# A two-layer graph kernel: a new order of work in the attention stage, and one pair's key rows gathered

## The chip, the cores and the metric

The kernel runs on one core of a Trainium2 chip. The metric is the device time of one execution in microseconds (us). A core has a matrix engine (PE, with its weight loads shown apart as PEld), a vector engine (DVE), a scalar engine (ACT), GpSimd (POOL), and a sync engine (SP) that here only issues transfers. Each works through its own list of instructions in order; they meet at semaphores.

## The reference

A graph of 3125 nodes with 256 features and 50,000 edges sorted by destination goes through two layers.

```python
h = relu(layernorm(x))
x = x + attention_layer(h)     # 8 heads of 32
h = relu(layernorm(x))
x = x + relation_layer(h)      # 8 relations
# attention_layer: q, k, v = layernorm(h) @ Wqkv + b
#   e = exp(q[src] . k[dst] - max),  agg = segment_sum(v[src] * e / sum(e), dst)
#   x1 = h + agg;  x1 + gelu(layernorm(x1) @ W_in + b_in) @ W_out + b_out
# relation_layer: sum over edges into dst of (h @ W[type])[src], + h @ loop_w + bias, gelu, layernorm
```

## The kernel before, in words

Nodes are cut into 25 blocks of 128. Edges are cut into 49 visits (`v`) of 1024, eight tiles of 128 edges; two tiles are a pair (`j` is 0 to 3). There are three stages, each a block of five instruction lists written out by hand. What stands in those lists sets the order of the work; there is no planner.

The first stage (to about 140 us) normalizes x, computes q, k and v for each block of nodes and writes tables to memory: `qv_tab` (q and v, float32, L263) and `k_tab` (the key cut into three bfloat16 parts, L265). DVE's `take` (L560) empties the products from PSUM, POOL's `split_keys` makes the three parts.

The second stage (about 140 to 1000 us) is the fused one, which the change is about. For each visit it does the edge work:
- POOL's `gather` (L1088): eight indirect transfers that fetch the q and v rows of the edges' sources. They wait until the same pair of the visit before last has been summed.
- PE's `keys(v, j)` (L1267): the key rows of a pair's destinations, by an indicator matrix times a window of 128 rows of `k_tab`, six bfloat16 matmuls into two PSUM banks. Pairs 0 and 2 use banks 0 and 1, pairs 1 and 3 banks 2 and 3, so each waits until the scores of the last user of its banks are ready.
- DVE: the product of q and key rows (L1500), its sum per head (L1505), `weigh` of the pair before (L1431, v times exponential) and `shift` (L1424). `to_window` (L1415) makes the indicators of the next visit.
- ACT's `weights(v, j)` (L1147, the exponentials), and `indicators` (L1138), which copies the indicators that PE's `turn` (L1257) has transposed.
- PE's `add_up(v, j)` (L1282) sums a pair into its window of nodes, `carry` (L1293) adds the last window's overlap, ACT's `take` (L1131) empties the result, SP stores it.

Into this the work on blocks of nodes is woven, one block `m` per two visits from visit 4 on. In even visit v = 4 + 2m (`hid`): DVE's `prepare` and `normalize` (L1440, L1459), PE's `turn_y`, ACT's `y_features`, PE's `hidden` in two halves (L1313), ACT's eight gelus in two halves (`gelu`, L1161). In odd visit v + 1 (`out`): PE's `feed` (L1325, the product with W_out), DVE's `statistics` (L1469) and `scale_of` (L1481), ACT's `relu` (L1170), PE's `turn_h1` (L1332), ACT's `h1_features` (L1180), then PE's `message` 0 to 3 (L1338, the products with eight relation matrices) and ACT's `keep_messages` (L1185). Messages 2 and 3 fall into the next even visit (`old`). ACT needs one table for the gelus and one for the exponentials; each change of table is an ACT_TABLE_LOAD. The lists of the two visits are in the loops at L1193 (ACT), L1351 (PE) and L1492 (DVE).

After visit 48 the last blocks are finished; a third stage (from about 1000 us) gathers the messages.

## Time and profile before

| what | value |
|---|---|
| median of three timed runs | 1618.47 us (1613.39 to 1624.01) |
| the profiled execution, its own time | 1609.75 us |
| its span in the trace | 1607.9 us |
| PE busy | 1168.3 us (73%) |
| DVE busy | 908.4 us (56%) |
| POOL busy | 889.5 us (55%) |
| ACT busy | 454.6 us (28%) |
| granted PE clock, mean | 0.876 of full |

Busy time is summed over the whole span, over stages with different limits. The chain of waits on the page follows only the end of the third stage, so the fused stage has to be read from its own rows.

### The profile page before, as it was taken

Reading aid. Unit: us, or ns where it says so; the run is one execution under the profiler, and the core shown is the slowest. Engines: PE = TensorE matmul, PEld = TensorE weight load, DVE = VectorE, ACT = ScalarE, POOL = GpSimd, SP = SyncE. Lnnn points to the kernel's source line nnn. Section 1 sums busy time; section 2 is a strip of 40 time slices with the busy share of each in tenths; the row PEclk is TensorE's granted clock in tenths of the full one; section 3 lists DMA queues with packets and bytes.
Section 4 is the critical chain, followed back from the end, with each engine's and each line's share of the span. In section 5 each row is a group of like instructions: output and inputs, shape, how many; then the busy total and the mean of one; then the engine's idle time right before and its main releaser. Section 6 shows DMA issues by size and latency. Waiting matters only on the chain. (4 is left out here: it accounts for less than half of the span.)

```text
span 1607.9 us, 18550 instructions
## 1 busy us (share of the span) xinstructions
PE 1168.3 (73%) x5463; PEld 864.7 (54%) x5463; DVE 908.4 (56%) x2801; ACT 454.6 (28%) x1150; POOL 889.5 (55%) x959
## 2 busy tenths in 40 slices
PE   5874579999899989999899988354565645553662
PEld 2443466777667766777667755233344424442452
DVE  5664577767777777777777662113434324533534
ACT  4652134443444443453444433000000000000000
POOL 2655656555555455555555510566676667666760
PEclk9997799999999999999999999687777767776776
DMA  6648666666667666566666611233343334433431
GB/s 203 157 132 265 208 200 201 205 222 202 207 197 233 206 210 188 189 223 189 203 191 220 194 46 57 79 108 106 113 125 114 114 106 121 119 115 109 121 114 51
DMA packets 137073, 255.68 MB, mean 159 GB/s; under 512 B 40426, under 2 KB 85460, under 8 KB 134026
## 3 DMA queue, kind: packets, MB, share of 16 engines
q0 software_dynamic: 50176, 154.19, 32.3%
q1 hardware_dynamic: 85834, 99.10, 19.0%
q10 hardware_dynamic: 960, 1.18, 0.2%
q8 instruction: 45, 0.74, 0.2%
q14 instruction: 58, 0.48, 0.1%
HBM read 192.76 MB, written 61.63 MB: 158 GB/s over the span
## 5 line engine op out<-in xcount | busy, mean ns | idle before, releaser
L1093 POOL DMA_INDIRECT arena<-qv_tab,srcs x392 | 391.8, 999 | 349.1 <-PE ps L1289 252.1
L1687 POOL DMA_INDIRECT arena<-h_all,typs x392 | 377.2, 962 | 210.3 <-issue 135.2
L1751 PE MATMUL ps<-arena 128*128 128x256 f32 x784 | 252.7, 482 | 114.8 <-DMA arena<-h_all,typs 49.9
L1289 PE MATMUL ps<-arena 128*128 128x264 f32 x784 | 221.2, 406 | 88.8 <-DVE arena L1437 49.9
L1751 PEld LDWEIGHTS ps<-arena 128*128 128x128 f32 x784 | 186.6, 246 | 176.1 <-issue 40.6
L1289 PEld LDWEIGHTS ps<-arena 128*128 128x128 f32 x784 | 140.2, 194 | 139.3 <-DVE arena L1437 66.8
L1500 DVE TENSOR_TENSOR arena<-arena,ps 128x512 f32<-128x512 f32 x196 | 134.3, 685 | 119.5 <-PE ps L1278 91.5
L1344 PE MATMUL ps<-wrel,arena 128*128 128x512 f32 x400 | 188.7, 598 | 1.7 <-ACT arena L1182 1.7
L1278 PE MATMUL ps<-arena 128*128 128x264 bf16 x1176 | 169.6, 282 | 12.6 <-DMA arena<-k_tab 11.0
L1278 PEld LDWEIGHTS ps<-arena 128*128 128x128 bf16 x1176 | 145.0, 145 | 41.4 <-issue 25.3
L1437 DVE TENSOR_TENSOR arena<-arena 128x512 f32<-128x512 f32 x196 | 134.0, 684 | 41.6 <-ACT arena L1150 40.9
L1505 DVE TENSOR_REDUCE arena<-arena 128x16 f32<-128x512 f32 x196 | 134.2, 685 | 5.1
L1804 DVE TENSOR_TENSOR arena<-ps,rowb 128x256 f32<-128x256 f32 x25 | 10.6, 425 | 223.7 <-remote 170.0
L1701 ACT ACTIVATE arena<-ps 128x256 f32<-128x256 f32 x49 | 18.7, 383 | 415.6 <-remote 286.5
L1150 ACT ACTIVATE arena<-arena,nbias 128x16 f32<-128x16 f32 x196 | 60.4, 308 | 196.4 <-DVE arena L1428 183.6
L1344 PEld LDWEIGHTS ps<-wrel,arena 128*128 128x128 f32 x400 | 73.1, 192 | 58.1 <-issue 52.4
L1189 ACT ACTIVATE arena<-ps 128x512 f32<-128x512 f32 x100 | 59.8, 598 | 137.9 <-PE ps L1344 125.0
L1328 PE MATMUL ps<-wout,arena 128*128 128x256 f32 x400 | 92.5, 385 | 6.0 <-issue 3.3
L1320 PEld LDWEIGHTS ps<-arena,win 128*128 128x128 f32 x800 | 93.0, 192 | 2.3 <-issue 0.5
L1788 DVE TENSOR_SCALAR arena<-dstf,wst 128x8 f32<-128x8 f32 x49 | 11.3, 230 | 145.9 <-ACT arena L1701 78.9
L1320 PE MATMUL ps<-arena,win 128*128 128x128 f32 (+1 forms) x800 | 93.2, 275 | 0.0
L1733 PE MATMUL ps<-ident,arena 128*128 128x128 f32 x50 | 14.8, 392 | 105.4 <-DVE arena L1799 82.5
(162 smaller groups left out, 1521.1 us busy)
## 6 DMA issues: line engine op xcount, KB each, us to landing
h_all<-arena SPq DMA_DIRECT2D x23, 1024.0 KB
arena<-dst SPq DMA_DIRECT2D x49, 256.0 KB
rel<-arena SPq DMA_DIRECT2D x77, 128.0 KB
arena<-k_tab SPq DMA_DIRECT2D x49, 198.0 KB
att<-arena SPq DMA_DIRECT2D x52, 132.0 KB, 6.0
qv_tab<-arena SPq DMA_DIRECT2D x25, 256.0 KB, 3.1
arena<-qv_tab,srcs POOLq DMA_INDIRECT x392
arena<-h_all,typs POOLq DMA_INDIRECT x392
```

Source lines behind the costliest of these rows:

```text
L1093: pool.indirect_dma_start(out=rowbuf[:, u * T + t, 0:2 * D], out_offset=None, in_=qv_tab, in_offset=bass.IndirectOffsetOnAxis(ap=srcs[:, v ...
L1150: nc.scalar.activation(rowbuf[:, at:at + 2, 2 * D:2 * D + H], sco[:, 2 * j:2 * j + 2, :], ACT.Exp, bias=nbias[:, :], scale=SCALE).then_inc ...
L1278: last = nc.tensor.matmul(ps[:, t % 4, 0:KW], tiles[:, t, :], kwin[:, u, c * KW:(c + 1) * KW], start=(c == 0), stop=(c == 2))
L1289: last = nc.tensor.matmul(ps[:, AGG, 0:AW], ind[:, v % 2, t, :], rowbuf[:, v % 2 * T + t, D:2 * D + H], start=(t == 0), stop=(v == 0 and t ...
L1320: last = nc.tensor.matmul(ps[:, (bank_y(m), bank_x(m))[half], n * P:n * P + wide_m], win[:, k, f * 128:(f + 1) * 128], yT[:, m % 2, k, 0:w ...
L1328: last = nc.tensor.matmul(ps[:, bank_y(m), 0:D], gT[:, m % 2, f, :], wout[:, f, :], start=(f == 0), stop=(f == FF // 128 - 1))
L1344: last = nc.tensor.matmul(ps[:, (bank_y(m), bank_x(m))[c % 2], :], h1T[:, m % 2, k, :], wrel[:, k, c * 512:(c + 1) * 512], start=(k == 0), ...
L1437: nc.vector.tensor_tensor(vals, vals, b[:, :, 2 * D:2 * D + H].unsqueeze(3).broadcast_to([EP, 2, H, DH]), ALU.mult).then_inc(w_ready, 1)
L1500: own.did(nc.vector.tensor_tensor(b[:, :, 0:D], b[:, :, 0:D], ps[:, bank:bank + 2, 0:D], ALU.mult))
L1505: own.did(nc.vector.tensor_reduce(sco[:, 2 * j:2 * j + 2, :], b[:, :, 0:D].rearrange("p t (h d) -> p t h d", d=DH), AX.X, ALU.add))
L1687: pool.indirect_dma_start(out=rowbuf[:, u * T + t, :], out_offset=None, in_=h_all[0:N * R, :], in_offset=bass.IndirectOffsetOnAxis(ap=typs ...
L1751: last = nc.tensor.matmul(ps[:, 6 + u, 0:D], ind[:, u, t, :], rowbuf[:, u * T + t, :], start=(t == 0), stop=(v == 0 and t == T - 1))
```

## The change

The fused stage's lists are written in another order, and the key rows of pair 1 of each odd visit no longer come from PE: POOL gathers them, float32, from a new table `kf_tab`, into a tile `kg`.

- First stage: `kf` (the ring of four key tiles) gets 8 more columns, which hold zeros, and SP stores each tile to `kf_tab` between the two stores that were there. `take` waits for all three stores of the block four before it, since the tile is now read by a store.
- PE: an odd visit is now add_up 0, add_up 1, feed, keys(next, 0), turn(next), add_up 2, keys(next, 1), add_up 3. The even visit begins with the odd visit's carry, then turn_h1 and messages 0 and 1; messages 2 and 3 follow in it. keys 2 and 3 of the next odd visit stand before the second half of `hidden`.
- ACT: the odd visit keeps only weights 2 and 3 and the indicators; its weights 0 and 1 stand in the even visit ahead of both gelu halves. relu, h1_features and all four messages stand in the even visit, as does the even visit's `take`, ahead of the gelus.
- DVE: prepare goes from pair 0 to 1, normalize from 1 to 2, statistics from 1 to 3. weigh of an odd visit's pair 3 stands between statistics and scale_of instead of in the next visit.
- POOL: two more gathers in each odd visit, behind the fourth row gather; the residual additions move in between the next visit's row gathers.

```diff
@@ stage 1: SP, DVE @@
                     sp.wait_ge(qkv_taken, 2 * b + 1)
                     sp.dma_start(qv_tab[b * P:(b + 1) * P, :], ...).then_inc(stored[j], 16)
+                    sp.wait_ge(qkv_taken, 2 * b + 2)
+                    sp.dma_start(kf_tab[b * P:(b + 1) * P, :], kf[:, b % NK, :]).then_inc(stored[j], 16)
                     sp.wait_ge(kl_ready, b + 1)
...
                     if b >= NK:
+                        dve.wait_ge(stored[(b - NK) % NST], 48 * ((b - NK) // NST) + 48)
@@ fused stage @@
+            def gathered(v, j):
+                return v % 2 == 1 and j == 1
@@ POOL, gather(v) @@
+                        if t % 2 and gathered(v, t // 2):
+                            gather_keys(v, t // 2)
+                        if t == 3 and v >= 1 and out_of(v - 1) is not None:
+                            residual(out_of(v - 1))
+                        if t == 5 and before(v):
+                            shift_result(before(v) - 1)
+
+                def gather_keys(v, j):
+                    if v >= 2:
+                        pool.wait_ge(k_used, PAIRS * (v - 2) + j + 1)
+                    for t in (2 * j, 2 * j + 1):
+                        pool.indirect_dma_start(
+                            out=kg[:, t % 2, :], out_offset=None, in_=kf_tab,
+                            in_offset=bass.IndirectOffsetOnAxis(ap=dsti[:, v * T + t:v * T + t + 1], axis=0)
+                        ).then_inc(kg_in, 16)
@@ ACT @@
+                    if v % 2:
+                        weights(v, 2)
+                        weights(v, 3)
+                        indicators(v + 1)
+                        continue
...
                     if v + 1 < G:
                         indicators(v + 1)
+                        weights(v + 1, 0)
+                    take(v)
+                    if v + 1 < G:
+                        weights(v + 1, 1)
                     if hid is not None:
                         gelu(hid, 0)
                         gelu(hid, 1)
@@ PE, keys(v, j) @@
+                    if gathered(v, j):
+                        return
...
+                    last_user = PAIRS * v + j - 2
+                    if last_user >= 0 and gathered(last_user // PAIRS, last_user % PAIRS):
+                        last_user -= 2
@@ DVE @@
+                def key_rows(v, j):
                     bank = 2 * (j % 2)
+                    return kg if gathered(v, j) else ps[:, bank:bank + 2, 0:KW]
...
-                        if out is not None and j == 1:
-                            statistics(out)
-                        if out is not None and j == 2:
-                            scale_of(out)
+                        if v % 2 and j == 3:
+                            if out is not None:
+                                statistics(out)
+                            weigh(v, 3)
+                            if out is not None:
+                                scale_of(out)
```

PE before, from the feed of an odd visit (L1328) on: L1278 is keys, L1289 add_up, L1263 turn, L1335 turn_h1.

```order
L1328 MATMUL ps<-wout,arena 128x256 [waits hidden_ready]
L1328 MATMUL ps<-wout,arena 128x256 x7
L1278 MATMUL ps<-arena 128x264 [waits scores_ready]
L1278 MATMUL ps<-arena 128x264 x5
L1289 MATMUL ps<-arena 128x264 [waits osum_ready,ind_ready,weighted_ready]
L1289 MATMUL ps<-arena 128x264
L1278 MATMUL ps<-arena 128x264 [waits scores_ready]
L1278 MATMUL ps<-arena 128x264 x5
L1289 MATMUL ps<-arena 128x264 [waits ind_ready,weighted_ready]
L1289 MATMUL ps<-arena 128x264
```

PE in the changed kernel, from the second half of hidden (L1356) in an even visit, through the odd visit: L1325 is add_up, L1364 feed, L1314 keys, L1294 turn.

```order
L1356 MATMUL ps<-arena,win 128x128 x8
L1325 MATMUL ps<-arena 128x264 [waits osum_ready,ind_ready,weighted_ready]
L1325 MATMUL ps<-arena 128x264
L1325 MATMUL ps<-arena 128x264 [waits ind_ready,weighted_ready]
L1325 MATMUL ps<-arena 128x264
L1364 MATMUL ps<-wout,arena 128x256 [waits hidden_ready]
L1364 MATMUL ps<-wout,arena 128x256 x7
L1314 MATMUL ps<-arena 128x264 [waits scores_ready,key_window_in0,indT_ready]
L1314 MATMUL ps<-arena 128x264 x5
L1294 MATMUL ps<-identb,arena 128x128 [waits ind_ready]
L1294 MATMUL ps<-identb,arena 128x128 x7
```

Two add_ups now stand between the hidden products and the feed, and keys 2 and 3 of the odd visit are gone from behind the feed. What follows in the changed kernel is the boundary to the even visit: L1337 is the carry, L1371 turn_h1, L1380 the messages.

```order
L1325 MATMUL ps<-arena 128x264 [waits ind_ready,weighted_ready]
L1325 MATMUL ps<-arena 128x264
L1337 MATMUL ps<-arena 128x264 [waits car_ready,osum_ready]
L1371 MATMUL ps<-ident,arena 128x128 [waits h1_ready]
L1371 MATMUL ps<-ident,arena 128x128
L1380 MATMUL ps<-wrel,arena 128x512 [waits h1T_ready]
L1380 MATMUL ps<-wrel,arena 128x512 x3
L1325 MATMUL ps<-arena 128x264 [waits osum_ready,ind_ready,weighted_ready]
```

There is now nothing on PE between the carry, turn_h1 and the first messages; before, a keys group and an add_up stood between turn_h1 and message 0.

ACT before, around the gelus (L1166): L1150 is an exponential, L1136 take, L1143 the indicators, L1174 relu.

```order
L1143 ACTIVATE arena<-ps 128x512 [waits summed,turn_ready]
L1143 ACTIVATE arena<-ps 128x512
L1166 ACT_TABLE_LOAD
L1166 ACTIVATE arena<-ps,bin_ 128x128 [waits hidden_psum]
L1166 ACTIVATE arena<-ps,bin_ 128x128 x3
L1166 ACTIVATE arena<-ps,bin_ 128x128 [waits hidden_psum]
L1166 ACTIVATE arena<-ps,bin_ 128x128 x3
L1150 ACT_TABLE_LOAD
L1150 ACTIVATE arena<-arena,nbias 128x2x8 [waits scores_ready]
L1136 ACTIVATE arena<-ps 128x264 [waits att_out,window_done]
L1150 ACTIVATE arena<-arena,nbias 128x2x8 [waits scores_ready] x2
```

The same place in the changed kernel (L1169 indicators, L1176 exponential, L1162 take, L1192 gelu).

```order
L1169 ACTIVATE arena<-ps 128x512
L1176 ACTIVATE arena<-arena,nbias 128x2x8 [waits scores_ready]
L1162 ACTIVATE arena<-ps 128x264 [waits att_out,window_done]
L1176 ACTIVATE arena<-arena,nbias 128x2x8 [waits scores_ready]
L1192 ACT_TABLE_LOAD
L1192 ACTIVATE arena<-ps,bin_ 128x128 [waits hidden_psum]
L1192 ACTIVATE arena<-ps,bin_ 128x128 x3
L1192 ACTIVATE arena<-ps,bin_ 128x128 [waits hidden_psum]
L1192 ACTIVATE arena<-ps,bin_ 128x128 x3
L1176 ACT_TABLE_LOAD
L1176 ACTIVATE arena<-arena,nbias 128x2x8 [waits scores_ready] x2
```

Two exponentials and the take moved from behind the gelus to ahead of them.

## Rows read from the trace of the kernel before

**Rows 1.** The page's head, and stretches: busy (instructions) per engine, PEclk, DMA share, GB/s.
```profile
span 1607.9 us, 18550 instructions
...
180.00:220.00 40.00, 25.81 (x139) 20.46 (x139) 29.89 (x69) 7.68 (x21) 24.85 (x27) 0.91 0.74 229
...
400.00:500.00 100.00, 90.62 (x509) 70.24 (x510) 74.90 (x202) 42.61 (x100) 55.51 (x58) 1.00 0.66 207
```

**Rows 2.** Timeline of PE, the hidden products of the second and the last pair of visits.
```profile
255.53 3.73 PE L1320 MATMUL ps<-arena,win 128*128 128x128 f32 x32
...
946.39 3.84 PE L1320 MATMUL ps<-arena,win 128*128 128x128 f32 x32
```

**Rows 3.** Timeline of PE, one pair of visits: start, length, line, [idle before <- releaser].
```profile
502.95 1.16 PE L1289 MATMUL ps<-arena 128*128 128x264 f32 x4 [1.67 <-issue]
503.94 0.38 PE L1335 MATMUL ps<-ident,arena 128*128 128x128 f32 x2
...
513.84 1.88 PE L1344 MATMUL ps<-wrel,arena 128*128 128x512 f32 x4
515.56 1.05 PE L1289 MATMUL ps<-arena 128*128 128x264 f32 x4
516.45 0.84 PE L1278 MATMUL ps<-arena 128*128 128x264 bf16 x6
517.12 0.38 PE L1310 MATMUL ps<-ident,arena 128*128 128x128 f32 x2
...
518.78 3.73 PE L1320 MATMUL ps<-arena,win 128*128 128x128 f32 x32
522.36 0.84 PE L1278 MATMUL ps<-arena 128*128 128x264 bf16 x6
...
524.80 3.72 PE L1328 MATMUL ps<-wout,arena 128*128 128x256 f32 x16 [0.27 <-ACT arena L1166]
...
531.77 1.16 PE L1289 MATMUL ps<-arena 128*128 128x264 f32 x4 [1.02 <-DVE arena L1437]
```

**Rows 4.** Timeline of DVE, the same pair of visits.
```profile
504.96 0.17 DVE L1444 TENSOR_SCALAR arena<-arena 128x8 f32<-128x8 f32 x1
...
509.41 0.15 DVE L711 TENSOR_SCALAR arena<-arena 128x1 f32<-128x1 f32 x1
...
512.93 0.68 DVE L1500 TENSOR_TENSOR arena<-arena,ps 128x512 f32<-128x512 f32 x1
...
514.25 0.68 DVE L1437 TENSOR_TENSOR arena<-arena 128x512 f32<-128x512 f32 x1
...
528.56 0.42 DVE L1473 TENSOR_TENSOR xs<-xs,ps 128x256 f32<-128x256 f32 x1 [0.99 <-PE ps L1328]
...
529.71 0.69 DVE L1500 TENSOR_TENSOR arena<-arena,ps 128x512 f32<-128x512 f32 x1
...
531.72 0.15 DVE L696 TENSOR_SCALAR arena<-arena 128x1 f32<-128x1 f32 x1
...
533.71 0.69 DVE L1500 TENSOR_TENSOR arena<-arena,ps 128x512 f32<-128x512 f32 x1
```

**Rows 5.** Timeline of ACT, the same pair of visits.
```profile
504.36 0.39 ACT L1182 ACTIVATE arena<-ps 128x256 f32<-128x256 f32 x1 [0.78 <-PE ps L1335]
...
522.56 2.18 ACT L1166 ACTIVATE arena<-ps,bin_ 128x128 f32<-128x128 f32 x8 [1.94 <-PE ps L1320]
524.76 1.28 ACT L1150 ACT_TABLE_LOAD   x1
...
535.59 0.60 ACT L1174 ACTIVATE arena<-xs,arena 128x256 f32<-128x256 f32 x1
```

**Rows 6.** Timeline of POOL, one row gather of the same pair of visits.
```profile
514.87 0.95 POOL L1093 DMA_INDIRECT arena<-qv_tab,srcs  x1 [0.30 <-issue]
```

**Rows 7.** The stores of `k_tab` in the first stage, from issue to landing.
```profile
DMA to landing us min/median/max: 1.9/2.3/4.0
```

**Rows 8.** Groups by line, 0 to 180 us: busy, mean ns | idle before <- releaser.
```profile
L568 DVE TENSOR_TENSOR arena<-ps,arena 128x512 f32<-128x512 f32 x25 | 17.3, 691 | 39.4 <-PE ps L473 39.4
```

More of the change, by code:

```diff
@@ L790, in program, with keys_before, keys_upto @@
             LASTM = hid_of(LASTV)
+            def gathered(v, j):
+                return v % 2 == 1 and j == 1
+            def keys_before(v):
+                return sum(not gathered(a, j) for a in range(v) for j in range(PAIRS))
+            def keys_upto(v, j):
+                return keys_before(v) + sum(not gathered(v, i) for i in range(j + 1))
             def x_of(m):
@@ L1220, in _ @@
                         gelu(hid, 1)
-                    if out is not None:
-                        h1_features(out)
-                        keep_h1(out)
-                take(LASTV)
                 relu(LASTM)
```

130 lines of the change are left out of this document (71 added, 59 removed).

## The prediction

> **What bounds the kernel now.** I read the stretches first [rows 1]. In the fused stage PE is busy 90.6 of 100 us at full granted clock, DVE 75, ACT 43, POOL 56, and the transfers take 0.66 of the DMA engines. So what can be won there is the tenth in which PE stands, and what PE no longer does. The period of two visits comes from the hidden products, which stand once per pair of visits: from the second to the last of them are 946.39 - 255.53 = 690.86 us over 21 pairs, 32.90 us each [rows 2].
>
> Then I read one pair on PE, from start to start [rows 3]. A message takes 1.72 (513.84 to 515.56), an add_up 0.89, a keys group 0.67, turn_y with turn and the next add_up 1.66, both hidden halves 3.58 (so 1.79 each); the feed is taken as the same, its row being as long. The carry is half an add_up, 0.44. The rows show three places where PE stands: 1.67 before the odd visit's add_up 2 (at 502.95), 1.02 before its add_up 1 (531.77), 0.27 before the feed (524.80). Together 2.96 us of 32.90; with the slower fill after each stop and the latency that the idle column doesn't count, some 4 us.
>
> DVE shows why [rows 4]. One step of a pair (product, sum, weigh, shift) is 512.93 to 514.25 plus 0.68 for weigh, 2.00. statistics costs 1.15 (528.56 to 529.71), scale_of 1.99 (531.72 to 533.71), normalize 3.52 (509.41 to 512.93), and prepare with one step and to_window 4.45 (504.96 to 509.41), so prepare and to_window 2.45. In the odd visit statistics stands ahead of pair 2's product and scale_of ahead of pair 3's. So weigh 1 ends at 531.72, just before PE's 531.77, and weigh 2 comes 1.99 later than its pair's data would allow. And all this hangs on the gelus: DVE's statistics starts 3.76 after the feed (528.56 - 524.80), and the feed waits for eight gelus of 2.18 that begin when the second hidden half is done [rows 3, 5]. The odd visit's first exponentials stand behind the gelus and a table load of 1.28 [rows 5].
>
> **The change part by part.**
>
> The gathered pair takes 0.67 us from PE in every odd visit. The reordering lets PE do both hidden halves, two add_ups (their exponentials stand before the gelus now) and then the feed, and it leaves DVE no statistics or scale_of in front of an odd pair. In return it puts a new chain at the head of the even visit: carry, turn_h1, messages 0 and 1 with nothing of PE's between, so PE waits there for DVE's scale_of and ACT's relu.
>
> I walk one pair of visits in the new order. Time 0 is the end of the odd visit's weigh 3.
>
> - scale_of 1.99 and 0.08 for its last small operation to end: 2.1. relu 0.60 [rows 5]: 2.7. turn_h1, from 503.94, has its result on ACT 0.42 later, h1_features 0.39 [rows 3, 5]: 3.6. PE has ended add_up 3 and carry at about 1.9, so it stands here for about 1.5 us in two pieces.
> - PE: messages 0 and 1, with 0.1 for the start, 3.7 to 7.2; add_up 0 to 8.1; keys 2, whose result is with DVE 0.84 + 0.1 later, at 9.0.
> - DVE has meanwhile done pairs 0 and 1, to_window and prepare: 2.0 + 1.6 (no weigh stands in pair 0) + 2.0 + 2.45 = 8.1. So it waits for PE until 9.0. Pair 2's step up to the end of weigh 1: 11.0. normalize: 14.55. Pair 3's step with weigh 2: 16.55.
> - PE did keys 3, message 2, add_up 1, the next keys 0, message 3 and the turns by 15.4 (turn_y waits a little for message 3 to be emptied, from the same bank). It then stands until 16.6 for add_up 2, which takes 1.0 after a stop: 17.6.
> - PE without a stop: hidden half 19.4, add_up 3 20.3, carry 20.7, two keys 22.05, hidden half 23.85, two add_ups 25.65.
> - ACT: exponentials of pair 0, take (after the carry, 20.9 to 21.3), exponential of pair 1 by 21.6, table load 1.28 to 22.9, four gelus at half of 2.18 to 24.0. The second half of hidden is with ACT at 24.0, so the last gelu ends at 25.1, half a microsecond before the feed could start. The reload of the other table and the exponential of pair 2 end at 26.8, under the feed.
> - feed 25.65; statistics 3.76 later, 29.4; 1.15 and weigh 3 0.68: 31.2. That is the next time 0.
>
> So a pair of visits takes 31.2 instead of 32.9 us, 1.7 less. PE's own work is 32.9 - 4.0 - 0.7 = 28.2 us of it; 3.0 us of standing remain, in other places (1.5 at the boundary, 1.2 before add_up 2, the rest small).
>
> A page of the skill speaks against this walk at the gelus. Here the table load at 524.76 follows the last gelu by 0.02 and takes 1.28 [rows 5]. The Trainium skill, ScalarE: Activation LUTs, section What ACT_TABLE_LOAD costs, gives about 1.28 us for the load and about 1.38 us more for a drain, 2.66 us per change of table. By that rule the last gelu would end at 26.5, past 25.65, and each pair would cost about 0.9 us more. The row shows no drain, and I go by it; the same delay from another cause is the first rival.
>
> The other costs:
> - The two key gathers are POOL's in each odd visit: 0.95 and 0.30 of issue each [rows 6], 2.5 us. With 16 row gathers and three additions POOL has about 25 of 31.2 us. They are asked for about 20 us before DVE needs them; without that cover each late us would stand on DVE.
> - Traffic grows by 256 rows of 1056 bytes, 0.27 MB per pair of visits, on 207 GB/s x 32.9 us = 6.8 MB [rows 1]. The rate becomes 7.08 MB / 31.2 us = 227 GB/s, the DMA share about 0.72. In 180 to 220 us the stage already ran at 229 GB/s and 0.74 [rows 1]. Cost zero; the other end is the last rival.
> - First stage: 25 more stores of 135 KB, and take waits for the stores of four blocks before. A k_tab store lands in 2.3, at most 4.0 us [rows 7], and take stands 39.4 us for PE over the stage [rows 8], so PE's pace hides the wait. I take 0.5 us; between 0 and 8 us, if a third of the blocks waited 1 us each.
> - Visits 0 to 3: rows arrive late there, and the two gathers of visit 1 push later ones back by up to 2.5 us, while exponentials no longer wait for indicators. I take 0, from -4 to +4. The first pair up to the second hidden product saves about 1 us more, like the others.
> - The end: in visit 48 ACT's take now stands before the gelus, so the table load starts only after the carry. Hidden half, add_up, carry (1.79 + 0.89 + 0.44, with 0.15 to the reader), take 0.4, load 1.28, gelus 2.18 are 7.1 us to the feed, where it was 5.1. This costs 2 us.
> - The third stage isn't touched: 0.
>
> Sum: 22 pairs (21 intervals between the second and last hidden products and the one before) x 1.7 = -37; +2 at the end, +0.5 in the first stage: -34.5 us. Against the profiled execution's 1609.75 us that makes 1575. The median of the three runs shown is 1618.47, 0.5% above it, so for a median I take 1618.5 - 34.5 = 1584.
>
> **The rivals.**
>
> *The gelus come too late.* Before, ACT stands for 1.94 us before 522.56, so from 520.6, and the first hidden half is done at about 520.8; yet the first gelu starts at 522.56, when the second half is done [rows 3, 5]. I can't name the cause of this hold. If it comes back, all eight gelus run from 24.0 to 26.2, the feed waits 0.6 and the pair takes 31.8: 22 x 1.1 = -24, with the small costs -22: 1597. If instead the last four are held 1.9 us, the feed starts at 27.1, the pair takes 32.7: no change that can be measured, about 1617. For: it is there in the old rows. Against: in the new order the first half's result lies ready 3 us before the gelu that reads it.
>
> *Only PE's work counts.* If DVE's results were in time everywhere, a pair would take PE's 28.2 and about 1 us of starts: 29.2, 22 x 3.7 = -81, with the small costs 1540. Against: the walk needs scale_of, relu and turn_h1 one after the other, by data, and nothing on PE stands there to cover them.
>
> *The stall only moves.* If the new boundary and the wait for normalize each cost 0.8 us more than the walk (PE slow to start after each of four stops, ACT's take or messages in the way), the pair takes 32.8, and all is within 1%: 1619. For: DVE has four long pieces now in a row on one loop. Against: each hand-over above is taken from a row.
>
> *The gathers bind, and it gets slower.* The transfers are one mechanism: 7.08 MB per pair must pass. If the stage can't move more than the 207 GB/s it moves now, the pair takes 34.2 us, row gathers land after DVE's need, and the kernel loses 22 x 1.3 = 29 us and the small costs: 1650. It costs time against before from 7.08 / 32.9 = 215 GB/s downwards. Against: 229 GB/s in 180 to 220 us [rows 1], and in the fused pair no product waits for rows.
>
> **How the numbers follow.** The walk holds with 0.64 (1584, its own range 1572 to 1594 by 0.4 us per pair and the bounds of the small costs). Gelus late, faster all the same: 0.14. Only PE's work: 0.04. Stall moved, or gelus held fully: 0.14. Gathers bind: 0.04. About 1% (16 us) is what a measurement of this kernel can tell from no change. Below 1602 lie the walk, the first rival's milder form and the PE case: 0.82. Within 1%: 0.14. Slower: 0.04. The range goes from 1560, some way toward the PE case, to 1608, which takes in the milder late gelus.
>
> **What would show it.** In the profile after: hidden products 31.2 us apart (33 or more would say that no step held); PE idle before turn_h1 and the first message some 1 to 1.5 us in all, and about 1.2 before the add_up behind turn_y; none before the odd visit's add_ups 1 and 2; the feed with next to no wait for a gelu. The feed waiting 0.5 us or more for ACT would be the first rival, DVE's products waiting for transfers the last. DVE's take in the first stage should show no wait for stores. The gathered product should take 0.69 like the others.

## The result and the profile after

The changed kernel takes 1628.74 us (median of 9 runs, 1621.80 to 1634.93), the kernel before 1618.96 in the same session. The ratio is 1.0065, interval 1.0044 to 1.0086: 0.65% slower, where 1584 us had been predicted. The profiled execution took 1626.97 us against 1609.75.

First the stretches, as in [rows 1]. Columns: busy time of PE, PEld, DVE, ACT, POOL, then the granted clock, the DMA share and GB/s. The last three lines cut the stretch behind one boundary finely, from turn_h1 through messages 0 and 1 to the keys behind them.

```profile
400.00:500.00 100.00, 91.88 (x494) 68.60 (x493) 75.69 (x198) 42.51 (x100) 62.84 (x64) 0.97 0.68 217
547.10:550.50 3.40, 2.56 (x6) 1.18 (x7) 2.97 (x8) 1.48 (x5) 2.50 (x3) 0.81 0.63 156
550.50:554.00 3.50, 3.50 (x8) 1.56 (x7) 1.04 (x3) 1.09 (x3) 0.82 (x1) 0.70 0.68 224
554.00:557.40 3.40, 3.40 (x20) 2.28 (x18) 1.91 (x4) 0.41 (x1) 1.89 (x2) 1.00 0.18 43
```

PE is busier than before (91.9 of 100 us), and yet nothing got faster: the granted clock of the stage is no longer 1.00 but 0.97. Within a pair it falls for a few microseconds and comes back; from 549.20 to 552.61 us it is 0.50, the lower of its two levels. Then the second and the last hidden product, the measure of [rows 2].

```profile
264.02 1.95 PE L1356 MATMUL ps<-arena,win 128*128 128x128 f32 x16
...
959.10 1.95 PE L1356 MATMUL ps<-arena,win 128*128 128x128 f32 x16
```

959.10 - 264.02 = 695.08 us over 21 pairs, 33.10 us each, where 32.90 was before and 31.2 predicted. (The last interval is short in both kernels, 29.90 and 31.88; without it the means are 33.26 and 32.95.) The mean hides two kinds of pair. Of the 21 intervals between the second halves of hidden, 15 lie between 33.7 and 34.0 us, the others between 30.7 and 33.2; the shortest, 503.37 to 534.13, is 30.76, less than the prediction's 31.2.

The timeline of all engines shows the boundary of a long pair. L1294 is turn, L1337 carry, L1537 the end of scale_of, L1169 the indicators' copy, L1200 relu, L1371 turn_h1, L1208 h1_features, L1124 a key gather. A "count" below is the update of a semaphore by which an engine tells the others that a result is there.

```profile
541.99 0.65 PE L1294 MATMUL ps<-identb,arena 128*128 128x128 bf16 x8
...
543.68 0.95 POOL L1124 DMA_INDIRECT arena<-kf_tab,dsti  x1 [0.30 <-issue]
...
544.99 0.61 PE L1337 MATMUL ps<-arena 128*128 128x264 f32 x2
545.15 0.16 DVE L1537 SCALAR_TENSOR_TENSOR arena<-arena 128x1 f32<-128x1 f32 x1
...
545.85 1.08 ACT L1169 ACTIVATE arena<-ps 128x512 f32<-128x512 bf16 x2 [5.37 <-remote]
...
546.82 0.60 ACT L1200 ACTIVATE arena<-xs,arena 128x256 f32<-128x256 f32 x1
...
547.47 0.44 PE L1371 MATMUL ps<-ident,arena 128*128 128x128 f32 x2 [1.87 <-ACT arena L1200]
...
547.95 0.38 ACT L1208 ACTIVATE arena<-ps 128x256 f32<-128x256 f32 x1 [0.25 <-PE ps L1371]
```

And PE alone, first this boundary, then that of the short pair (L1380 is message):

```profile
547.47 0.44 PE L1371 MATMUL ps<-ident,arena 128*128 128x128 f32 x2 [1.87 <-ACT arena L1200]
548.38 5.40 PE L1380 MATMUL ps<-wrel,arena 128*128 128x512 f32 x8 [0.47 <-ACT arena L1208]
...
515.32 0.44 PE L1371 MATMUL ps<-ident,arena 128*128 128x128 f32 x2 [0.43 <-ACT arena L1200]
516.24 3.70 PE L1380 MATMUL ps<-wrel,arena 128*128 128x512 f32 x8 [0.47 <-ACT arena L1208]
```

Read ACT's line at 545.85 with care. Of what ACT waits for there, only turn's result is recent, and by its row turn ended at 542.64. The count by which PE tells of it is recorded at 545.82, together with those of add_up 2, keys 1, add_up 3 and the carry (all within 545.8 to 546.1). ACT works in order, so relu, whose data were ready at 545.3, starts at 546.82, 1.5 us late. PE stands 1.87 and 0.47 us instead of 0.43 and 0.47, and then its clock falls: the same eight matmuls take 5.40 us instead of 3.70. 1.4 and 1.7 are 3.1 us, the difference of the two kinds of pair.

The waits from 300 to 930 us say how often (columns: engine, line <- what it waited for: us in total, times, longest). Both occur once per pair, in 17 and 15 of the 19 pairs there.

```profile
ACT arena L1169 <- remote: 90.1, 17, 5.6
...
PE ps L1371 <- ACT arena L1200: 27.3, 15, 2.1
```

The rest of the loss stands at the ends. The first hidden product starts at 230.20 instead of 223.25, 7.0 us later. The end:

```profile
962.22 1.95 PE L1356 MATMUL ps<-arena,win 128*128 128x128 f32 x16
...
966.35 3.72 PE L1364 MATMUL ps<-wout,arena 128*128 128x256 f32 x16 [2.18 <-ACT arena L1192]
```

From the last hidden product to its feed are 966.35 - 959.10 = 7.25 us, where it was 951.47 - 946.39 = 5.08. The sum: 7.0 at the start, 5.8 in 22 pairs, 2.2 at the end, and 1.2 behind it, 16.2 us; the spans differ by 16.1 (1624.0 and 1607.9).

### The profile page after: what moved, and what is told of

The parts are those of the page before. It is cut to its first block and busy times, and to the rows that moved or that the text cites. A ratio compares the mean times of both kernels' runs of the same rounds, so it can differ in the third digit from the quotient of the medians.

```text
span 1624.0 us, 18336 instructions
## 1 busy us (share of the span) xinstructions
PE 1190.7 (73%) x5319; PEld 860.8 (53%) x5319; DVE 916.4 (56%) x2801; ACT 453.4 (28%) x1150; POOL 948.4 (58%) x1008
## 5 line engine op out<-in xcount | busy, mean ns | idle before, releaser
L1109 POOL DMA_INDIRECT arena<-qv_tab,srcs x392 | 397.9, 1015 | 284.2 <-PE ps L1325 186.3
L1325 PE MATMUL ps<-arena 128*128 128x264 f32 x784 | 216.2, 404 | 33.1 <-DVE arena L1487 19.4
L1380 PE MATMUL ps<-wrel,arena 128*128 128x512 f32 x400 | 214.3, 677 | 12.1 <-ACT arena L1208 12.1
L1325 PEld LDWEIGHTS ps<-arena 128*128 128x128 f32 x784 | 141.0, 195 | 82.0 <-DVE arena L1487 40.2
L1487 DVE TENSOR_TENSOR arena<-arena 128x512 f32<-128x512 f32 x196 | 145.0, 740 | 54.2 <-ACT arena L1176 48.5
L1552 DVE TENSOR_TENSOR arena<-arena,ps 128x512 f32<-128x512 f32 x172 | 117.0, 680 | 102.4 <-PE ps L1314 74.9
L1314 PE MATMUL ps<-arena 128*128 128x264 bf16 x1032 | 143.6, 285 | 12.9 <-DMA arena<-k_tab 12.8
L1314 PEld LDWEIGHTS ps<-arena 128*128 128x128 bf16 x1032 | 126.8, 146 | 31.0 <-issue 15.3
L1380 PEld LDWEIGHTS ps<-wrel,arena 128*128 128x128 f32 x400 | 80.8, 216 | 98.7 <-issue 80.2
L1176 ACT ACTIVATE arena<-arena,nbias 128x16 f32<-128x16 f32 x196 | 59.9, 306 | 163.0 <-DVE arena L1478 125.6
L1356 PE MATMUL ps<-arena,win 128*128 128x128 f32 (+1 forms) x800 | 96.9, 275 | 0.0
L1356 PEld LDWEIGHTS ps<-arena,win 128*128 128x128 f32 x800 | 94.9, 192 | 2.3 <-ACT arena L1183 0.6
L1364 PE MATMUL ps<-wout,arena 128*128 128x256 f32 x400 | 92.5, 385 | 2.2 <-ACT arena L1192 2.2
L1169 ACT ACTIVATE arena<-ps 128x512 f32<-128x512 bf16 x98 | 53.0, 595 | 129.0 <-remote 107.3
```

Of the source, the lines that this page charges most:

```text
L1109: pool.indirect_dma_start(out=rowbuf[:, u * T + t, 0:2 * D], out_offset=None, in_=qv_tab, in_offset=bass.IndirectOffsetOnAxis(ap=srcs[:, v ...
L1176: nc.scalar.activation(rowbuf[:, at:at + 2, 2 * D:2 * D + H], sco[:, 2 * j:2 * j + 2, :], ACT.Exp, bias=nbias[:, :], scale=SCALE).then_inc ...
L1314: last = nc.tensor.matmul(ps[:, t % 4, 0:KW], tiles[:, t, :], kwin[:, u, c * KW:(c + 1) * KW], start=(c == 0), stop=(c == 2))
L1325: last = nc.tensor.matmul(ps[:, AGG, 0:AW], ind[:, v % 2, t, :], rowbuf[:, v % 2 * T + t, D:2 * D + H], start=(t == 0), stop=(v == 0 and t ...
L1356: last = nc.tensor.matmul(ps[:, (bank_y(m), bank_x(m))[half], n * P:n * P + wide_m], win[:, k, f * 128:(f + 1) * 128], yT[:, m % 2, k, 0:w ...
L1364: last = nc.tensor.matmul(ps[:, bank_y(m), 0:D], gT[:, m % 2, f, :], wout[:, f, :], start=(f == 0), stop=(f == FF // 128 - 1))
```

## The experiments

The runs came to more than one chip. Before takes 1618 us beside e1 to e4, 1508 beside e5 to e8, and 1608 beside the others, so ratios to before on the same chip are compared. "Pair" is the distance of the hidden products from the second to the last by 21; "start" is where the first one begins. Both are of the one profiled execution, while the ratio is of medians.

| run | ratio to before | pair, us | start, us |
|---|---|---|---|
| changed kernel | 1.0065 [1.0044, 1.0086] | 33.10 | 230.2 |
| e1 relu first | 0.9809 [0.9780, 0.9838] | 30.92 | 228.7 |
| e2 filled | 0.9942 [0.9916, 0.9967] | 32.04 | 233.1 |
| e3 no gather | 0.9798 [0.9756, 0.9839] | 31.18 | 226.1 |
| e4 gather alone | 1.0065 [1.0036, 1.0093] | 33.12 | 230.3 |
| e5 turn early | 0.9863 [0.9847, 0.9880] | 31.02 | 211.2 |
| e6 late gather | 0.9754 [0.9737, 0.9770] | 30.47 | 204.6 |
| e7 stores alone | 0.9999 [0.9986, 1.0013] | 32.26 | 204.5 |
| e8 all | 0.9738 [0.9722, 0.9755] | 30.48 | 203.8 |
| e9 changed kernel again | 1.0065 [1.0041, 1.0089] | 32.31 | 232.3 |
| e10 before again | one run, 1610.15 us | 32.84 | 223.2 |
| e11 turn early again | 1.0008 [0.9976, 1.0040] | 32.54 | 232.1 |
| e12 keys last | 0.9924 [0.9900, 0.9948] | 31.63 | 230.2 |
| e13 fetched, unused | 1.0184 [1.0145, 1.0224] | 33.47 | 225.4 |
| e14 all again | 0.9723 [0.9696, 0.9751] | 30.58 | 222.0 |
| e15 order without gather | 0.9767 [0.9749, 0.9785] | 31.18 | 222.4 |
| e16 changed kernel, third time | 1.0034 [1.0000, 1.0067] | 32.61 | 233.6 |

**e1: relu ahead of the copied indicators**

```diff
@@ ACT, odd visit @@
-                        indicators(v + 1)
+                        if before(v + 1) is None:
+                            indicators(v + 1)
                         continue
@@ ACT, even visit, behind take @@
                     if old is not None:
                         h1_features(old)
+                        indicators(v)
```

> The changed kernel, with ACT's order altered at one place: the indicators of an even visit stand behind relu, take and h1_features instead of ahead of relu. Theory (clock): in most pairs of visits the copied indicators are released some 3 us late, relu stands behind them and comes 1.5 us late, PE stands 1.9 us before turn_h1, and the granted clock then falls to half for messages 0 and 1. Then this kernel has every pair at about 30.8 us like the few undisturbed ones (503.37 to 534.13), no stretch below full clock between 300 and 900 us, and is about 22 x 2.3 = 50 us faster than the changed kernel: near 1578 us, ratio to before about 0.975. Rival (chain): scale_of, relu and turn_h1 alone are long enough a stand to lower the clock: pairs stay at 33 to 34 us, 1629 us, ratio 1.006. Rival (gathers): the gathered pair's transfers and DVE's reads of them cost the time: ACT's order changes nothing, 1629 us.

```profile
524.42 0.44 PE L1373 MATMUL ps<-ident,arena 128*128 128x128 f32 x2 [0.40 <-ACT arena L1200]
525.33 3.70 PE L1382 MATMUL ps<-wrel,arena 128*128 128x512 f32 x8 [0.47 <-ACT arena L1208]
```

In PE's timeline of e1 every boundary is like the short pair's, the clock is 1.00 from 300 to 900 us, and the pair is 30.92. So the lateness of relu starts it. The stage ends 48 us earlier than in the changed kernel (last hidden product at 910.78), as expected; the whole came out at 1587 and not 1578, because what lies behind the last hidden product is 7.6 us longer in the profiled execution (672.5 against 664.9). Why stays open; the changed kernel itself has 664.8 there in e9 and 671.1 in e16, so much of it may be scatter. PE's counts are as late as before (up to 3.4 us), but nothing that leads to relu waits for them any more.

**e2: the stand filled**

```diff
@@ PE, even visit @@
+                        fill(v, old, 6)
                         turn_h1(old)
+                        fill(v, old, 4)
                         message(old, 0)
```

> The changed kernel with ten additional matmuls per pair of visits, 128x264, whose result nobody reads: six between the carry and turn_h1, four between turn_h1 and message 0. ACT's order is the changed kernel's, so relu stays late. Theory (clock): PE no longer stands long enough there, the granted clock stays full, eight message matmuls take 3.7 us instead of 5.4, and a slow pair goes from 33.85 to about 32.2 us, the good ones lose up to 0.5: 22 x 0.9 to 1.3 = 20 to 28 us faster than the changed kernel, about 1605 us. If the lower clock is only a companion of the lateness and costs nothing by itself, no gain: 1629 us or, where the added matmuls push turn_h1 back, up to 10 us more.

```profile
508.89 0.44 PE L1371 MATMUL ps<-ident,arena 128*128 128x128 f32 x2 [1.41 <-ACT arena L1200]
509.17 0.61 PE L1378 MATMUL ps<-arena 128*128 128x264 bf16 x4
509.81 3.70 PE L1386 MATMUL ps<-wrel,arena 128*128 128x512 f32 x8
```

The fill adds useless work and leaves out nothing. relu is late as before (turn_h1 still waits 1.41 us behind six of the fills, at 506.64), but the messages take 3.70, the clock is 1.00, and the pair goes from 33.10 to 32.04. So the two costs come apart: about 1.1 us per pair from the clock, another 1.1 (32.04 to 30.92) from the lateness itself. The medians say nearly the same: 0.0123 and 0.0133 of before's 1618 us, 0.9 and 1.0 us for each of 22 pairs.

**e3 and e4: without the gathered pair, and the gathered pair alone**

```diff
@@ e3: changed kernel, stores and wait gone @@
             def gathered(v, j):
-                return v % 2 == 1 and j == 1
+                return False
@@ PE, even visit @@
                     add_up(v, 2)
+                    if v + 1 < G:
+                        keys(v + 1, 1)
@@ e4: kernel before, with stores, wait and, on POOL @@
+                        if t % 2 and gathered(v, t // 2):
+                            gather_keys(v, t // 2)
```

> The changed kernel without the gathered pair: keys 1 of the odd visit comes from PE again, behind the even visit's add_up 2, and the 25 stores of the float32 keys and the wait for them are gone. Theory (clock): the gathered pair isn't where the time went, so a pair of visits costs up to 0.7 us more for the six matmuls of PE, less 3 us in the first stage and at the start of the fused one: 1629 to 1642 us. Rival (gathers): its transfers, POOL's two issues and DVE's slower reads cost more than they bring: this kernel is faster than the changed one by 10 us or more, 1619 or less, with pairs of 32.5 us or less.

> The kernel before with the gathered pair alone (stores, wait and two gathers per odd visit), its order otherwise kept. Theory (clock): the gather by itself is harmless and takes 0.67 us from PE in each pair of visits where PE was at work: between 0 and 15 us faster, less 3 us at the start, 1606 to 1622 us, ratio 0.992 to 1.002. Rival (gathers): the transfers or DVE's reads beside them slow the stage, pairs go above 32.9 us, ratio 1.005 or more, 1627 us or above.

Both went the rival's way. e3 is 2.7% faster than the changed kernel. Its timeline (L1106 row gather, L1291 turn, L1166 indicators, L1197 relu) tells why:

```profile
518.78 0.95 POOL L1106 DMA_INDIRECT arena<-qv_tab,srcs  x1 [0.30 <-issue]
...
519.61 0.65 PE L1291 MATMUL ps<-identb,arena 128*128 128x128 bf16 x8
...
520.73 1.09 ACT L1166 ACTIVATE arena<-ps 128x512 f32<-128x512 bf16 x2 [2.92 <-PE ps L1291]
...
523.35 0.60 ACT L1197 ACTIVATE arena<-xs,arena 128x256 f32<-128x256 f32 x1 [1.53 <-issue]
```

PE's order around turn is the changed kernel's, but turn's count comes 0.44 us after turn's end and not 3.2, and relu has nothing in front of it. POOL's run of four gathers ended at 519.73, 1.0 us before. In the changed kernel the run is six long and ends at 544.63, 1.2 us before the counts. In the kernel before, the run ended at 521.60 and the first gelu, which [rows 5] shows standing 1.94 us, started at 522.56, 1.0 us behind it. That made the next theory. Gathers alone (e4) gain nothing: PE loses the keys that stood between hidden and feed, and in the pair shown the feed waits for the gelus 1.16 us where [rows 3] had 0.27. The rival was right in its numbers for both; its cause, transfers and DVE's slower reads, was not what the next runs showed.

```profile
532.52 1.06 PE L1321 MATMUL ps<-arena 128*128 128x264 f32 x4
533.42 0.61 PE L1333 MATMUL ps<-arena 128*128 128x264 f32 x2
535.19 3.72 PE L1360 MATMUL ps<-wout,arena 128*128 128x256 f32 x16 [1.16 <-ACT arena L1193]
```

**e5 to e8: turn early, gathers later, stores alone, all mended**

```diff
@@ e5: PE, odd visit @@
                         add_up(v, 1)
+                        turn(v + 1)
                         if out is not None:
                             feed(out)
                         keys(v + 1, 0)
-                        turn(v + 1)
@@ e6: e1 and @@
-                return v % 2 == 1 and j == 1
+                return v % 2 == 1 and j == 1 and v >= 5
...
@@ e7: kernel before, nobody reads kf_tab @@
+                    sp.wait_ge(qkv_taken, 2 * b + 2)
+                    sp.dma_start(kf_tab[b * P:(b + 1) * P, :], kf[:, b % NK, :]).then_inc(stored[j], 16)
...
@@ e8: e6 and, ACT @@
-                    take(v)
                     if v + 1 < G:
+                        take(v)
                         weights(v + 1, 1)
...
+                take(LASTV)
```

> The changed kernel with one PE step moved: in the odd visit, turn for the next visit stands ahead of the feed instead of behind the feed and the next keys 0. ACT's order is the changed kernel's, so the copied indicators stand ahead of relu. In the changed kernel ACT starts them 0.25 us after the carry has ended, 3.2 us after turn has, and PE's counts for turn, add_up 2, keys 1 and add_up 3 all arrive then. If a count of turn's is delayed by the place it has in PE's list (what stands between it and the next stop), it should come in time here, since the feed's own count does: ACT's indicators start before the exponential of pair 3 is done or right behind it, relu is on time, pairs of 30.8 us, 1578 to 1590 us, no stretch below full clock. If any count of turn's is kept until PE stops, wherever it stands, the indicators again start behind the carry: pairs of 33 to 34 us, 1629 us.

> Kernel e1 (relu ahead of the indicators) with the gathered pair only from visit 5 on; visits 1 and 3 take pair 1's keys from PE. The first hidden product starts at 230.2 us in the changed kernel and the kernel with the gather alone, 228.7 in e1, 226.1 without gather and stores, 223.3 before. If the gathers of visit 1 and 3 are what delays the start (rows late), the first hidden product comes at 226 or earlier here and the kernel is 2 to 4 us faster than e1, 1584 us. If the stores in the first stage do it, it stays at 228 to 229 and the kernel at 1587 us.

> The kernel before with the 25 stores of the float32 keys and take's wait for them alone; nothing reads them. The trace says it, not the time: first fused gather at 141.05 us and first hidden product at 223.25 before, 143.78 and 230.20 in the changed kernel. If the stores make the first stage longer, the first gather is issued at 143 to 144 us here; if they cost nothing, at 141. The first hidden product then comes at 224 to 226 (stores) or 223 to 224. Time within 0.3% of before, 1619 to 1622 us.

> Kernel e6 with one more edit: the last visit's take stands behind the gelus again. The prediction gave that place 2 us: from the last hidden product to the feed behind it are 7.25 us in the changed kernel (959.10 to 966.35) and 5.08 before. Here they should be 5.1 again, and the kernel 2 us faster than e6, between 1580 and 1585 us, ratio to before 0.977 to 0.980. If the take there costs nothing, it is as long as e6.

These four came to the other chip. There no count of PE's that the traces record is late, so e5 could not decide its question, though it looked as if it had. e7: the stores cost nothing (0.9999). POOL's first gather of the fused stage is issued between 140.3 and 144.2 us in all these runs, with the stores or without, so the 2.7 us between 141.05 and 143.78, from which the expectation set out, are scatter. e6 and e8 start at 204, e5, with the gathered pair from visit 1 on, at 211: having it in visits 1 and 3 costs the start. e8's end:

```profile
877.02 1.95 PE L1359 MATMUL ps<-arena,win 128*128 128x128 f32 x16
880.20 3.72 PE L1367 MATMUL ps<-wout,arena 128*128 128x256 f32 x16 [1.23 <-ACT arena L1192]
```

873.90 to 880.20 is 6.30 us, in e6 it is 7.25, and in e7, with the old order, 5.07. The take costs 0.95 there; the other 1.2 are put down to the add_up and the carry that now stand between the two halves of hidden (0.89 and 0.44), which no run took out. In e6 PE stands 2.18 us before this feed and the clock falls: the feed takes 5.41 us, in e8 3.72. The changed kernel stood the same 2.18 and its feed took 3.72, so the length of one stand does not decide alone.

**e9 to e11: the changed kernel, before, and e5 once more**

> The changed kernel once more, without an edit. The runs e1 to e4 came from a chip on which PE's counts arrive late in batches, as in the traces of before and after; in the traces of e5 to e8, from another chip (before takes 1508 us there), each count of PE's that the trace shows arrives 0.01 us after its matmul. Theory (late counts): on a chip like the second the changed kernel has pairs of about 31.0 us and full clock without any edit, ratio to before 0.984 to 0.988, because before's pair is 32.3 there; on a chip like the first it is again at 33 us per pair and 1.005 to 1.008. Rival (order alone): the ratio is 1.005 to 1.008 on either chip, since ACT's order and the clock do it without late counts.

> The kernel before, without an edit, for its trace on the same chip. Late counts cost it too: the last gelus' wait for the second half of hidden. On a chip where counts are in time its pair of visits should be 32.3 us, as in e7, and the gelus should start before the second half is done; on one with late counts 32.9.

> Kernel e5 (turn ahead of the feed) again, beside the changed kernel on the same chip. Where counts arrive late: if the place in PE's list decides, ACT's indicators start within the feed's time, relu is on time and the ratio to before is 0.978 to 0.985; if a count of turn's is kept until PE stops, 1.005. Where counts arrive in time: e5 and the changed kernel agree within 0.3%, and e5's gain is not its own.

The first two are without an edit, the third is e5's kernel. This chip has late counts. The changed kernel repeats its 1.0065, with fewer long pairs (32.31 in the mean) and a later start (232.3 against 223.2). Its profiled execution, 1612.93 us, is 5 us under its median, and in it the pairs are even shorter than before's 32.84 (e10): what it loses there it loses at the start. e10's 32.84 is what was expected where counts are late; e7, the old order where they are in time, has 32.26. e11 answers what e5 could not, and by neither expectation. The indicators are copied in time, during the feed. But in many pairs now the count of the carry comes late instead (L1162 is take, L1208 h1_features):

```profile
317.46 0.44 PE L1371 MATMUL ps<-ident,arena 128*128 128x128 f32 x2 [0.95 <-issue]
317.62 0.95 POOL L1109 DMA_INDIRECT arena<-qv_tab,srcs  x1 [0.30 <-issue]
319.83 0.39 ACT L1162 ACTIVATE arena<-ps 128x264 f32<-128x264 f32 x1 [2.43 <-remote]
...
320.55 1.07 PE L1380 MATMUL ps<-wrel,arena 128*128 128x512 f32 x1 [2.65 <-ACT arena L1208]
```

PE had ended the carry at 316.5 and turn_h1 at 317.9 and stood. The counts came at 319.8, 1.2 us after POOL's last gather of a run of eight from 308.3 to 318.6. So PE's stop doesn't release them, and turn isn't special. The kernel takes 1.0008 of before, where the changed one has 1.0065 and, in e16, 1.0034.

**e12 and e13: the run of gathers made shorter, and longer again**

```diff
@@ e12: changed kernel, POOL @@
-                        if t % 2 and gathered(v, t // 2):
-                            gather_keys(v, t // 2)
+                        if t == 7 and gathered(v, 1):
+                            gather_keys(v, 1)
@@ e13: e3 with stores and gathers, DVE takes PE's keys @@
+                        if fetched(v, j):
+                            dve.wait_ge(kg_in, 32 * (v // 2) + 32)
+                        dve.wait_ge(k_ready, keys_upto(v, j))
```

> The changed kernel with POOL's two key gathers moved from behind the fourth to behind the eighth row gather of the odd visit's rows. Theory (bursts): on chips like the first, counts of PE's are held while POOL issues a close run of gathers and come about 1.2 us after the last issue of the run has ended (409.6 to 414.5, counts at 415.8; in e3, without key gathers, 515.0 to 519.7, counts at 520.7; in the kernel before 516.9 to 521.6, count at 522.5). With two gathers less in that run it ends 2.5 us earlier, turn's count comes at about 413.3, the indicators don't push relu back, the clock stays full: pairs of 30.8 to 31.5 us, ratio to before 0.975 to 0.985. Rival (no link with POOL): pairs stay at 33 us, ratio 1.006.

> Kernel e3 (keys 1 of the odd visit from PE) with the stores and the two key gathers of the changed kernel put back behind the fourth row gather; DVE waits for their rows but takes the keys of PE. Theory (bursts): the run of gathers is as long as in the changed kernel again, turn's count comes 3 us late again, relu with it, and most pairs go from 31.25 to between 33 and 34.5 us; with 6 us more at the start the kernel is 1625 us or more, ratio 1.003 or more. Rival (PE's work): if it was PE's missing keys group, not POOL's gathers, that changed the timing, this kernel is like e3: ratio 0.980, plus 0.004 for the start.

```profile
499.33 0.95 POOL L1109 DMA_INDIRECT arena<-qv_tab,srcs  x1 [0.30 <-issue]
...
500.14 0.66 PE L1294 MATMUL ps<-identb,arena 128*128 128x128 bf16 x8
...
501.17 1.09 ACT L1169 ACTIVATE arena<-ps 128x512 f32<-128x512 bf16 x2 [2.54 <-PE ps L1294]
...
504.19 0.44 PE L1371 MATMUL ps<-ident,arena 128*128 128x128 f32 x2 [0.43 <-ACT arena L1200]
```

With the run two gathers shorter (e12, above) turn's count comes 0.4 us after turn, PE stands 0.43, the clock is 1.00. The gain is smaller than expected, 31.63 us per pair and ratio 0.9924 where 0.975 to 0.985 was said: its start, 230.2, is still the late one, and the two gathers now lengthen a run later in the even visit, where DVE's product waits for keys 2 (1.11 us at 510.65; 39.8 us in 20 waits from 300 to 930 us, where e1 has 16.8). e13 (below; L1127 key gather, L1172 indicators, L1374 turn_h1) does PE's work as e3 does it, and the two gathers and the stores make it 3.9% slower than e3 by their ratios, with clock 0.95 from 300 to 600 us:

```profile
512.53 0.95 POOL L1127 DMA_INDIRECT arena<-kf_tab,dsti  x1 [0.30 <-issue]
...
514.05 1.08 ACT L1172 ACTIVATE arena<-ps 128x512 f32<-128x512 bf16 x2 [5.00 <-issue]
...
515.67 0.44 PE L1374 MATMUL ps<-ident,arena 128*128 128x128 f32 x2 [1.21 <-ACT arena L1203]
516.58 5.40 PE L1383 MATMUL ps<-wrel,arena 128*128 128x512 f32 x8 [0.47 <-ACT arena L1211]
```

Here turn had ended at 511.51, 2.5 us before the copy started. From 300 to 930 us no wait of e13's DVE is put down to a transfer, so it isn't the fetched rows' landing that makes the kernel slow. So a long run of POOL's gathers delays the counts, on these chips. Part of e13's expectation failed: its start is 225.4, not 6 us later than e3's 226.1 (another chip), though 3.0 later than that of e15, without any key gather on e13's chip. With the gathered rows also used it is 229 to 234 on these chips. So the greater part of the late start comes only when DVE takes them. The mechanism wasn't tried. On the other chip transfers have a share: from 145 to 232 us DVE waits 11.9 us for rows of `qv_tab` in e5 and 7.4 in e6, and in e5 0.69 and 0.44 for key rows.

**e14 to e16: the best version, the order without the gather, the changed kernel**

e14 is e8's kernel and e16 the changed one, without an edit. e15 is e3 with the edits of e1 and with e8's take:

```diff
@@ ACT, e15 @@
-                        indicators(v + 1)
+                        if before(v + 1) is None:
+                            indicators(v + 1)
...
+                take(LASTV)
```

> Kernel e8 (relu ahead of the indicators, key gathers from visit 5 on, last take behind the gelus) again, if possible on a chip with late counts: 1587 (e1) less 5 for the start less 2 for the end, 1580 us, ratio 0.976 to 0.978; on a chip like the one of e8, 0.974.

> Kernel e3 (no gathered pair, no stores) with relu ahead of the indicators and the last take behind the gelus: what the new order is worth without the gathered pair. Pairs of 31.2 us as in e3, since relu was in time there already; 2 us less at the end: 1585 us on a chip like the first, ratio 0.978 to 0.980. So beside e14 the gathered pair would be worth 0.5 us per pair, 0.5 to 0.7% in all.

> The changed kernel unedited, in hope of a chip like that of e5 to e8, where PE's counts are in time. There e5 had pairs of 31.07 us and e7, whose order is that of before, 32.3. Theory (late counts): the changed kernel has pairs of about 31 us and full clock there, ratio to before 0.984 to 0.988, since the only thing that keeps it from the predicted 31.2 is the late count. If the order alone is at fault, pairs of 33 us and 1.005 to 1.008. On a chip with late counts 1.005 to 1.008 by either.

```profile
255.74 1.95 PE L1359 MATMUL ps<-arena,win 128*128 128x128 f32 x16
...
897.86 1.95 PE L1359 MATMUL ps<-arena,win 128*128 128x128 f32 x16
```

e14 is 2.8% faster than before and 3.1 to 3.4% faster than the changed kernel (1.0034 and 1.0065) by their ratios, on a chip with late counts, a little more than expected. Its counts are as late as the changed kernel's (up to 3.3 us), yet its clock is 1.00 from 300 to 900 us: the mended order doesn't make them come sooner, it keeps them off the path. On the chip where no count is late the same kernel had 0.9738. e15 has the same order and no gathered pair: 31.18 against 30.58 us per pair, 0.9767 against 0.9723. So with the order mended the gathered pair is worth 0.6 us per pair, close to the 0.67 of PE's work that it takes away. e16 came to a chip with late counts again and only repeats a loss, a smaller one (1.0034, its interval beginning at 1.0000). That the changed kernel would gain where counts are in time was therefore not shown; e5, one step from it, had 0.9863 there.

## Why the prediction was wrong

- **The walk of one pair** was right for a pair in which nothing is late: 30.76 in the changed kernel's own short pair, 30.92 in e1, against 31.2. Its 1.7 us of gain per pair would have come out as 2.0. That is in part luck: PE stands 1.44 us in the short pair (0.43, 0.47, 0.28, 0.26), where the walk had 3.0, so PE's own part was taken about 1.1 us too small, and the two errors nearly cancel.
- **The step that failed** is "scale_of 1.99 and 0.08 [...] relu 0.60: 2.7". It let relu start when its data are there. ACT's list has the copied indicators ahead of relu in the odd visit, and the walk has no entry for them, though the description of the change and its diff show them there. They wait for turn, and turn's count is late. relu started 1.5 us after its data in a long pair, and that costs 1.1 us per pair in the mean (e2 to e1).
- **The clock was never priced.** The prediction noted "full granted clock" before, created a boundary at which PE stands twice with one short turn_h1 between, and kept all durations at full clock. With relu late the clock fell, 1.1 us per pair net (changed kernel to e2). In the rows, stands of 1.87 and 0.47 lowered it, as did 1.21 and 0.47 in e13, and stands of 0.43 and 0.47 did not. Of the 50.6 us between forecast and trace (34.5 less forecast, 16.1 more measured), 43 lie in the 22 pairs.
- **The hold was seen and put in the wrong place.** The first rival named the 1.94 us that ACT stood before the gelus for no visible reason and let it come back only at the gelus, for 0.14. The gelus were not late (the feed doesn't wait). The same lateness struck at turn, because the change itself made POOL's run of gathers longer there (e12, e13). The rival "the stall only moves" gave 1619, near the 1628.7, with two waits 0.8 us longer each than in the walk. The first came: PE stands 1.87 and 0.47, 2.34 us, at the boundary of a long pair, where the walk had 1.5. The other, the wait for normalize, did not: PE stands 0.26 before that add_up (528.66), where 1.2 was predicted. The messages' 1.70 us at the lower clock, which that rival didn't have, stand in its place, so its number is near partly by luck. The gathered product takes 0.68, as said.
- **The gathers** bind by no rate: e14 moves 231 GB/s from 400 to 500 us, where the rival named 215 as the point from which it costs time. Their price was in time, not traffic: "The other costs" counted their 2.5 us on POOL as hidden, and did not ask what else moves with POOL's run.
- **Small terms.** First stage 0.5: nothing measurable (e7), and take waits for PE alone, 40.3 us as 39.4 in [rows 8]. Start 0, from -4 to +4: 7.0, outside its own bounds. End 2: 2.2, but only 0.95 of it is the take (e6 to e8). Third stage 0: 1.2, less than it varies from one execution of the changed kernel to another (6.3 between e9 and e16).
- **The page weighed** in the prediction, the Trainium skill, ScalarE: Activation LUTs, section What ACT_TABLE_LOAD costs, would have a drain of 1.38 us beside each load. Here the last gelu ends at 537.70 and the load starts at 537.72 and takes 1.28, and the exponential behind it starts at 539.02, as in the row of before: no drain on either side.

What stays open is why a run of gathers holds PE's counts, why one chip doesn't do it, and why in the short pair turn's count came alone at 513.68, a little before the run's last issue had ended (513.92), while those of add_up 2, keys 1, add_up 3 and the carry came from 515.15 to 515.33, 1.2 us and more behind it. The link with POOL is shown by e12 and e13, the exact rule is not.

## What to carry to other kernels

Walk each engine's list in order and give every instruction ahead of a critical one an entry, also those that look free: a copy that waits for another engine passes its lateness on to all behind it. Where the rows show a result taken up late for no visible reason, as the gelus here, look at what the other queues do at that moment and price the same lateness at every hand-over of the new order. And where a change puts two stands of PE close together, price the lower clock for what follows.

## What the runs showed of the hardware

Counts of PE's can reach the other engines more than 3 us late (545.82 for 542.64 in the changed kernel), several at once, while POOL issues indirect gathers one right after another. Most come 0.9 to 1.5 us after the end of the run's last issue, some inside the run. In e3, e12 and e15, with a run of four there, turn's count comes at most 0.6 us after turn; in the changed kernel, with a run of six, it comes 2.5 to 3.4 us after turn in 18 of the 19 pairs in which it is recorded late (230 to 930 us). On the chip of e5 to e8 the counts came 0.01 us after the end that the profile gives for their matmul. The Trainium skill, Perfetto Trace Analysis, section Tensor Engine Instruction, says that a matmul's end in a profile is estimated from its size and that the count is sent once PSUM has acknowledged all bytes. A late acknowledgement would fit that, but no run here shows it.

DVE's small subtraction (shift) of the gathered pair takes six times as long as that of the others (changed kernel, groups by line, 230 to 960 us: count, busy, mean ns; the first form reads PSUM, the second SBUF alone):

```profile
L1478 DVE TENSOR_TENSOR arena<-arena,ps 128x16 f32<-128x16 f32 x154 | 25.2, 163 | 0.8
L1478 DVE TENSOR_TENSOR arena<-arena 128x16 f32<-128x16 f32 x22 | 20.7, 941 | 0.0
```

One of POOL's additions stands beside it (from 502.02 for 0.74 us, the shift from 501.83 for 0.98). In e4, where POOL does nothing at that moment (504.36), the same shift takes 0.17, as in the mean of all 22 there (169 ns). The Trainium skill, SBUF — State Buffer, section SBUF: two separate sides, has the rule: a DVE operation with two SBUF inputs and a GpSimd operation that reads SBUF exclude each other. The numbers agree with that, though the rows can't tell which of the two had the access first. It is 0.78 us per pair on DVE, and e14, the fastest version, has it too; what taking it away would bring wasn't tried.
